# A retention stage's pairs overlapped: the next pair's norm, turns and projections among a pair's score masks, and the group norm's root on GpSimd

## What is computed

```python
q = (x @ W_Q) ...; k = (x @ W_K) ...; v = (x @ W_V) ...      # 8 heads of 16
decay = jnp.where(causal, jnp.exp(diff * jnp.log(gammas)), 0.0)
scores = jnp.einsum('bhtd,bhsd->bhts', q, k) / jnp.sqrt(16.)
out = jnp.einsum('bhts,bhsd->bhtd', scores * decay, v)
g = (g - mean) / jnp.sqrt(var + EPS)                         # group norm over each head's 16
```

## Time and profile before

| | us |
|---|---|
| median of 3 runs | 2267.86 (2266.97 to 2274.65) |
| span of the profiled execution, first to last instruction (its own time; nothing more is recorded around it) | 2301.6 |
| PE busy | 1858.3 |
| DVE busy | 1747.6 |
| ACT busy | 1317.0 |
| POOL busy | 327.8 |
| retention stage, first query product to last residual | 387.6 to 582.7 |

### The profile page before, as it was taken

One profiled execution on the slowest core, in us unless ns is written; L12 is line 12 of the kernel. 1 busy time (PEld: TensorE's weight loads), 2 busy tenths in 40 slices (PEclk: granted clock), 3 DMA queues, 4 the chain that ended last, 5 costly groups with the idle time before them and its releaser, 6 DMA issues. The chain is left out here.

```text
span 2301.6 us, 31594 instructions
## 1 busy us (share of the span) xinstructions
PE 1858.3 (81%) x11676; PEld 957.7 (42%) x11676; DVE 1747.6 (76%) x4911; ACT 1317.0 (57%) x1459; POOL 327.8 (14%) x392
## 2 busy tenths in 40 slices
PE   5998998988766688999999999889999888652930
PEld 2565755766421123344433334433344553231620
DVE  3667557667777789999999999999999789763532
ACT  0223122231237999999999999999999612100310
POOL 6000022010343000000000000000000000173256
PEclk9879999787777999999999999999999999776975
DMA  5501000000001100000000000000000000221632
GB/s 163 180 1 38 16 2 14 1 1 1 1 0 35 65 1 1 1 1 1 1 1 1 1 1 1 1 1 1 1 1 1 1 1 0 106 92 53 208 96 73
DMA packets 39658, 67.08 MB, mean 29 GB/s; under 512 B 7744, under 2 KB 27728, under 8 KB 38736
## 3 DMA queue, kind: packets, MB, share of 16 engines
q1 hardware_dynamic: 30768, 41.96, 5.4%
q0 software_dynamic: 8736, 23.10, 3.2%
HBM read 39.87 MB, written 23.07 MB: 27 GB/s over the span
## 5 line engine op out<-in xcount | busy, mean ns | idle before, releaser
L1942 ACT ACTIVATE KM<-KM 128x2048 f32<-128x2048 f32 x290 | 538.9, 1909 | 8.0 <-DVE KM L1765 8.0
L1765 DVE TENSOR_SCALAR KM<-big 128x512 f32<-128x512 f32 x1160 | 480.8, 484 | 38.7 <-PE bank L2080 32.9
L2080 PE MATMUL bank<-KM,w_a_wa 128*32 128x512 f32 x2736 | 379.6, 629 | 91.1 <-ACT KM L1942 69.7
L189 POOL TENSOR_TENSOR nrstd<-nrstd,minus_half 128x4 f32<-128x4 f32 (+1 forms) x80 | 82.4, 1050 | 1745.9 <-DVE nrstd L166 1745.5
L1942 ACT ACTIVATE aa_args<-aa_args 128x2048 f32<-128x2048 f32 x142 | 266.1, 1909 | 1.5 <-DVE aa_args L1765 1.5
L1765 DVE TENSOR_SCALAR aa_args<-big 128x512 f32<-128x512 f32 x568 | 236.3, 484 | 13.8 <-PE bank L2080 13.2
L2080 PE MATMUL bank<-aa_args,w_a_wa 128*32 128x512 f32 x1360 | 188.2, 627 | 42.2 <-ACT aa_args L1942 28.5
L2080 PEld LDWEIGHTS bank<-KM,w_a_wa 128*32 128x32 f32 x2736 | 54.8, 109 | 243.0 <-ACT KM L1942 140.6
L2052 PE MATMUL bank<-XT,rf_wgu 128*128 128x256 f32 x512 | 143.9, 404 | 0.0
L2046 PE MATMUL bank<-XT,rf_wgu 128*128 128x256 f32 x512 | 142.2, 400 | 0.8 <-DVE ST L1837 0.8
L1939 ACT ACTIVATE KM<-big 128x512 f32<-128x512 f32 x208 | 132.8, 717 | 0.0
(11 more groups left out here) (405 smaller groups left out, 3120.6 us busy)
## 6 DMA issues: line engine op xcount, KB each, us to landing
queues<-zeros SPq DMA_DIRECT2D x1, 8192.0 KB, 24.1
KM<-queues SPq DMA_DIRECT2D x32, 256.0 KB, 3.0
results<-KM POOLq DMA_DIRECT2D x32, 256.0 KB, 3.4
w<-in_w SPq DMA_DIRECT2D x1, 4096.0 KB
big<-in_w_pairs SPq DMA_DIRECT2D x1, 4096.0 KB
mf_tv<-in_task_W SPq DMA_DIRECT2D x1, 2048.0 KB, 10.4
la_v<-in_task_W SPq DMA_DIRECT2D x1, 2048.0 KB, 8.6
big<-XN SPq DMA_DIRECT2D x8, 256.0 KB, 2.7
```

The source lines that it names most:

```text
L189: self.nc.gpsimd.tensor_tensor(self.m.nrstd[s][:, 0:self.tiles], self.m.nrstd[s][:, 0:self.tiles], self.m.minus_half[:, 0:self.tiles], ALU ...
L1765: last = nc.vector.tensor_scalar(ARG(n, step)[:, cc, :], KU[:, i * T:(i + 1) * T], q, None, ALU.add)
L1942: last = nc.scalar.activation(ARG(n, step), ARG(n, step), ACT.Tanh)
L2080: last = nc.tensor.matmul(m.bank[g][32 * cc:32 * cc + 32, :], w["a_wa"][:, 30 - 2 * k:62 - 2 * k], ARG(n, step)[:, cc, :], start=k == 0, s ...
```

## The change

The norm statistics of the next pair but one are computed after a pair's query and key products, its scaling among the masks. PE turns and projects the next pair between scores; the gate inputs and the projection move among the next pair's scores; `attend` of the first sequence stands between the scores of units 4 and 5. Query products have two buffers (`QPS`), since those of the next pair are written while this pair's second `attend` still reads. GpSimd computes the power -0.5 of the 128x64 variances in place of ScalarE's `Sqrt` and DVE's reciprocal.

```diff
-    QP = [m.KM[s][:, 0:2, :].rearrange("p b t -> p (b t)") for s in S]
+    QPS = [[m.KM[s][:, 2 - 2 * k:4 - 2 * k, :].rearrange("p b t -> p (b t)") for s in S] for k in range(2)]
+    QP = lambda i, s: QPS[i % 2][s]
...
+            def group_root(i):
+                pool.wait_ge(var_sb.sem, var_sb.at(i, 2))
+                nc.gpsimd.tensor_tensor(gvar[:, :], gvar[:, :], m.minus_half[:, 0:2 * N8], ALU.pow).then_inc(root.sem, 1)
...
             front(0)
-            states(0)
+            front_norm(1)
+            for c in range(NS):
+                states(0, c)
...
+                    masks(i, (1, 2))
+                    if i:
+                        residual(i - 1)
+                    masks(i, (3,))
+                    if i:
+                        gate_stats(i - 1)
+                    masks(i, (4,))
+                    norm.vector_scale(dve, i, norm.pair(i + 1), XN)
+                    masks(i, (5,))
+                    if i:
+                        gate_scale(i - 1)
+                    masks(i, (6, 7))
+                    front(i + 1)
+                    if i + 2 < PAIRS:
+                        front_norm(i + 2)
...
-                nc.vector.reciprocal(gvar[:, :], gvar[:, :]).then_inc(rstd.sem, 1)
...
+                    states(i + 1, 0)
+                    normed(i, 0)
+                    states(i + 1, 1)
+                    normed(i, 1)
+                    states(i + 1, 2)
+                    gated(i)
...
-                nc.scalar.activation(gvar[:, :], gvar[:, :], ACT.Sqrt).then_inc(root.sem, 1)
...
+                    scores(i, (1,))
+                    if i:
+                        project(i - 1)
+                    scores(i, (2, 3, 4))
+                    attend(i, (0,))
+                    scores(i, (5, 6))
+                    turn(i + 1)
+                    scores(i, (7,))
+                    if i:
+                        turn_b(i - 1)
+                    variances(i, (0,))
+                    keys(i + 1)
+                    attend(i, (1,))
+                    if i:
+                        logits(i - 1)
+                    variances(i, (1,))
+                    values(i + 1)
+                    widen(i, (0,))
+                    states(i + 1, 0)
+                    widen(i, (1,))
+                    states(i + 1, 1)
+                    states(i + 1, 2)
```

More of the change, by code:

```diff
@@ L1058, in front @@
                     for par in range(2):
[L1059 removed]
+                        last = nc.vector.tensor_tensor(by_par(QP(i, s))[:, :, par, :], by_c(QB[s][:, :]), by_c(w[f"decay_q{par}"][:, :]), ALU.mult)
                     last.then_inc(q_sb.sem, 1)
@@ L1168, in _ @@
             front(0)
-            states(0)
+            front_norm(1)
+            for c in range(NS):
+                states(0, c)
             for i in range(PAIRS):
[L1171 to L1177, removed]
+                last = i + 1 == PAIRS
+                masks(i, (0,))
+                if i:
+                    activated(i - 1)
+                if last:
+                    residual(i - 1)
                     for u in range(len(UNITS)):
-                        masks(i, (u,))
+                        if u:
+                            masks(i, (u,))
                         for part in range(6):
@@ L1183, in _ @@
                     ranked(0, 1)
+                else:
+                    masks(i, (1, 2))
+                    if i:
+                        residual(i - 1)
+                    masks(i, (3,))
[10 more added lines that the diff above has]
+                        front_norm(i + 2)
                 for s in S:
@@ L1307, in _ @@
             for i in range(PAIRS):
-                for s in S:
-                    act.wait_ge(av_ps.sem, av_ps.at(i, s + 1))
-                    nc.scalar.activation(SQ[s], OB[s][:, :], ACT.Square).then_inc(sq_sb.sem, 1)
-                    nc.scalar.activation(Y[s], OB[s][:, :], ACT.Copy, scale=w["gn"][:, 0:1]).then_inc(y_sb.sem, 1)
+                if i:
+                    gates(i)
+                squares(i, 0)
                 if i + 1 < PAIRS:
@@ L1519, in _ @@
             values(0)
-            states(0)
+            for c in range(NS):
+                states(0, c)
             for i in range(PAIRS):
-                nxt = i + 1 < PAIRS
-                if nxt:
-                    scores(i, range(len(UNITS)))
-                    attend(i)
-                    turn(i + 1)
-                else:
-                    for u in range(len(UNITS)):
+                scores(i, (0,))
+                if i:
+                    gate_inputs(i)
+                if i + 1 == PAIRS:
+                    project(i - 1)
+                    columns(0, 0)
+                    for u in range(1, len(UNITS)):
                         scores(i, (u,))
```

170 lines of the change are left out of this document (95 added, 75 removed).

## The result

| | before | after |
|---|---|---|
| median, same chip, 6 runs each | 2271.82 (2266.97 to 2281.39) | 2290.24 (2288.80 to 2294.99) |
| ratio, 95% interval | | 1.0086 [1.0072, 1.0101] |
| span of the profiled execution | 2301.6 | 2288.6 |
| stage, first score mask of pair 0 to last residual | 181.35 | 203.2 |
| POOL busy in the program | 327.8 | 370.5 |

The change costs 18.4 us by the medians. The forecast of 2251 us, a gain of 16.8, was wrong, and its sign too; 2290 also lies above its range, which ended at 2280. On a second chip the same two kernels gave 1.0102 [1.0059, 1.0145].

The account below looks back on a forecast made before the run. Neither DVE nor TensorE was full; they handed over to each other in series. Pairs 0 to 3 changed by -9.0, -6.8, -6.2 and +5.2 us, total -16.8, so 2267.9 became 2251 us, range 2236 to 2280.

Parts of the forecast that it names:

- R: GpSimd's time for the 128x64 power of the variances, once per pair: taken as 3 us, between 1.17 and 16.6.
- rival B: Slower by the power alone, GpSimd working column by column, R up to 16.6 us; chance 0.22 together with rival D.
- Rival A: The power costs hardly more than for four columns, R of 1.1 to 2 us: 2245 us, chance 0.21.
- rival D: New waits (c) and (d), 5 to 7.5 us, replace the old ones: 2268 us; chance 0.22 together with rival B.
- (a): DVE's new wait for unit 2's scores, which stand behind the gate inputs and the projection: 1.3 us.
- (b): DVE's wait for unit 5's scores, behind the first sequence's attend: 2.0 us in pair 0, 0.5 later.
- (c): DVE's wait for the second variance behind keys, attend and logits: 2.0, 2.2 and 4.5 us in pairs 0 to 2.
- (d): DVE's wait for GpSimd's root behind the second variance: nearly all of R, where before DVE did not wait.
- (e): Wait of the first state mask for spread, widening and state: 1.0 us, and 0.2 for the next.
- three such signs: Prediction wrong if power over 7 us, stage clock lower than before, or attend waits ahead of unit 5 over 3 us.
- table loads: Eight ScalarE loads of 1.28 us go; priced at nothing, as ScalarE is idle 9.02 us before the Tanh behind them.
- loss by the clock: A rival: attend and keys among the scores run at half clock, about 10 us in three pairs: 2261; chance 0.13.

Follow-up runs that it names:

- e6: The change with GpSimd's power on only 16 of the 64 columns: ratio 0.9938 to the kernel before, stage 168.0 us.
- e3: The kernel before with powers of 1 to 64 columns and one multiplication added on idle GpSimd, run once: stage 178.5 us.
- e8: The change with the root on ScalarE and DVE, one sequence at a time, and four queue moves: ratio 0.9974 to the kernel before, stage 175.4 us.
- e10: The change with the root on ScalarE and DVE and the projection after unit 2's scores: ratio 0.9917 to the kernel before, stage 160.6 us.
- e1: The change with the root back on ScalarE and DVE: ratio 0.9935 to the kernel before, 0.9923 when repeated, stage 165.9 us.

## Why the prediction was wrong, step by step

**The step that failed** is the size of R: "I take 3 us, some fifteen times the add's slope", chosen between bounds of 1.17 and 16.6. It measured 10.55, and that term alone turns the sign. Under it lay a misread row: "The 128x2 power took 1.11 us against 1.04 for 128x4, so up to four columns the count hardly matters, and most of the time is fixed". Both were means over the whole program, the first over powers of 1.14 and of 0.70 us. The single 128x2 row of 0.70 us would have put R at 9.9, 0.1 under the prediction's own point for 0.5% slower. The choice "nearest in kind to the 128x4 row" had no size in it: the piece of work asked for has sixteen times its columns. The Trainium skill's figure (GPSIMD Engine Reference, 3.1 Elementwise), read as covering a power, gave R near 1.2; the measurement decides, and says that it doesn't cover it.

**The mechanism held, the slope nearly.** "Each us over 3 costs 4 us": it was 3.9 above 10.55 us, and 4.6 from 2.90 to 10.55. With R = 10.55 the prediction's own sum is -16.8 + 30.2 = +13.4 us. This is rival B's mechanism. It had 0.5% slower begin at R = 10.0; R came at 10.55 and the program 0.9% slower, a case to which the prediction had given 0.14. Rival A (R under 2) and rival D (a sum of zero near R = 7) fell with the same number.

**The rest of the sum, at R = 10.55**, is 8.4 us short of the stage's +21.8 (and 5.0 of the medians' +18.4). All in us:

| term | predicted | measured in the change |
|---|---|---|
| DVE busy, pairs 0, 1, 2 | 23.1, 30.6, 28.2 | 22.9, 29.8, 27.4 |
| pair 0, ahead of units 2 and 4 | 1.6 | 1.97 |
| (a) ahead of unit 2, pairs 1, 2 | 1.3 | 1.76 |
| (b) ahead of unit 5 | 2.0, 0.5, 0.5 | 3.24, 0, 0 |
| (c) second variance | 2.0, 2.2, 4.5 | 2.25, 2.45, 4.80 |
| (d) root | R | 10.66, 10.5, 10.5 |
| (e) state masks | 1.2 | 3.3, 3.3, 3.2 |
| ahead of the queries | 0 | 0.65, 0.1, 0.1 |

Right in place and near in size: the busy times, (a), (c), and pair 3 (54.05 + 7.55 = 61.6 against 62.4). (b) in pair 0 lies inside its bounds of 1.2 to 3.7 and was taken too low. It is also over the 3 us that the prediction had set as a sign of being wrong; of its three such signs two came, this one and the power over 7 us, and the third did not (mean granted clock of the stage 0.79, before 0.77). (e) is the one that broke: 2.0 us too little three times over, since TensorE's clock fell to half during the long wait. It is mostly not a separate error, as e6 shows (1.4, 1.8 and 1.4 us with a short power), but a second price of R that the straight slope of 4 left out.

**Right too:** norm waits for GpSimd gone, the logits' wait gone, table loads worth nothing, no loss by the clock among the scores at large (pairs 1 and 2 of the change: mean 0.89 against 0.85 before). With R near 3 the forecast would have been off by 3.8 us in the stage (e6: -13.4, where R = 2.90 gives -17.2).

## What to carry to other kernels

A count that grows sixteenfold needs a slope, not a neighbour: take two sizes of the same operation, each from single rows and never from means over the program, and draw the line through them before choosing inside wide bounds. An operation that sits in a chain on which two engines wait is priced as often as the chain runs; here TensorE's half clock behind a wait of 10.55 us came on top. Filling an idle microsecond of the vector engine is no gain if it takes one from TensorE ahead of dense matmuls.

## What the runs showed of the hardware

- GpSimd's power costs 0.15 to 0.16 us per column of 128 partitions over about 0.4 us (e3, 2 to 64 columns), thirty-three times a multiply of the same tile at 64 columns (10.55 against 0.32 us). ScalarE's `Sqrt` of it takes 0.26 us and DVE's reciprocal 0.55.
- The same 128x2 power takes 1.14 us in some stretches and 0.70 in others; why is open.
- Idle time right before a matmul doesn't tell the clock behind it: 2.59 us were followed by nearly 10 us at half clock (e8), 1.26 us ahead of an attend by full clock (e10), and 1.08 us ahead of the same attend by half clock (e1).
- In the change the granted clock fell to half during a TensorE wait of 8.88 us; behind a wait of 1.23 us at the same place it was full (e6).
- Unchanged code behind the stage took 1694.9 us in one execution of a kernel and 1717.4 in another, a difference as large as the effect studied.
